# Experts' output rows scattered to their token's place by the experts' pass, and plain reads in the two combines

## The reference

```python
x = x + gnn_0(layernorm(x), edge_attr, src, dst, ...)     # gather, segment sum, MLP
x = x + moe_0(layernorm(x))    # 16 experts, 256 -> 512 -> 256, ReLU, two choices, then a layer norm
x = x + gnn_1(layernorm(x), src, dst, ...)                # dense product, 32 largest kept, mean over neighbours
x = x + moe_1(layernorm(x))    # 8 experts, 256 -> 256 -> 256, GELU, two choices
```

```python
h = act(x @ w1[e] + b1[e]);  y = h @ w2[e] + b2[e]
out = x + w_first * y_first + w_second * y_second
```

## Time and profile before

| | before |
|---|---|
| median of the runs | 2162.16 us (2155.62 to 2167.88) |
| span of the profiled execution | 2148.3 us, mean granted TensorE clock 0.786 |
| PE, PE weight load, VectorE busy | 1334.0, 1159.6, 730.7 us |
| ACT, Pool busy | 427.2, 1088.9 us |
| packets on Pool's software queue | 48192, 131.35 MB, 21.6% of 16 engines |
| packets on SP's hardware queue | 178994, 154.64 MB, 22.3% of 16 engines |
| expert pass e0 | 816 to 1073 us |
| combine and dense product m0 | 1073 to 1262 us |
| expert pass e1 | 1909 to 2062 us |
| last combine o1 | 2062 us to the end |

### The profile page before, as it was taken

The page is one execution under the profiler, slowest core; times in us unless marked ns, Lnnn a source line. Parts: engine busy times, 40 slices in busy tenths (PEclk is TensorE's granted clock), DMA queues, the critical chain, the costliest instruction groups (busy, mean ns, idle before and its releaser), DMA issues. The chain is left out here.

```text
span 2148.3 us, 31218 instructions
## 1 busy us (share of the span) xinstructions
PE 1334.0 (62%) x7997; PEld 1159.6 (54%) x7998; DVE 730.7 (34%) x2198; ACT 427.2 (20%) x1492; POOL 1088.9 (51%) x1144
## 2 busy tenths in 40 slices
PE   0467778788778727999946534454555555358820
PEld 0456667777667716999812224454454454357720
DVE  4123334434434552111169931222222222341123
ACT  0001111111111202444344400000000000114433
POOL 2655556655555103222187746666666666233355
PEclk9878887877888858999956677667677766679975
DMA  5333333333333107999822223333333333139955
GB/s 169 103 99 101 101 99 107 109 97 103 103 100 105 35 8 270 354 349 351 279 82 80 68 64 88 91 96 96 98 88 94 94 97 87 42 112 320 318 175 155
DMA packets 230143, 289.43 MB, mean 135 GB/s; under 512 B 76686, under 2 KB 181152, under 8 KB 229782
## 3 DMA queue, kind: packets, MB, share of 16 engines
q1 hardware_dynamic: 178994, 154.64, 22.3%
q0 software_dynamic: 48192, 131.35, 21.6%
q10 hardware_dynamic: 2852, 2.24, 0.4%
HBM read 256.41 MB, written 32.04 MB: 134 GB/s over the span
## 5 line engine op out<-in xcount | busy, mean ns | idle before, releaser
L726 POOL DMA_INDIRECT O0G<-n_rows,O0idx x392 | 384.2, 980 | 309.1 <-ACT O0idx L721 203.4
L726 POOL DMA_INDIRECT O1G<-sparse_rows,O1idx x392 | 376.7, 961 | 214.4 <-issue 108.2
L739 PE MATMUL O1ps_sums<-O1OH,O1G 128*128 128x128 f32 x1568 | 280.4, 347 | 148.6 <-DVE O1OH L744 84.1
L739 PEld LDWEIGHTS O1ps_sums<-O1OH,O1G 128*128 128x128 f32 x1568 | 259.5, 256 | 163.1 <-DVE O1OH L744 91.0
L739 PE MATMUL O0ps_sums<-O0OH,O0G 128*128 128x128 f32 x1568 | 243.5, 317 | 34.3 <-DMA O0G<-n_rows,O0idx 16.1
L739 PEld LDWEIGHTS O0ps_sums<-O0OH,O0G 128*128 128x128 f32 x1568 | 229.7, 230 | 39.9 <-issue 39.7
L758 DVE TENSOR_TENSOR sumT<-sumT,O1ps_sums 128x256 f32 x98 | 41.3, 421 | 421.6 <-DMA m0own<-token_rows 307.3
L1331 POOL DMA_INDIRECT e0xs<-token_rows,e0idx x64 | 60.5, 946 | 206.2 <-ACT e0idx L1391 205.1
L758 DVE TENSOR_TENSOR sumT<-sumT,O0ps_sums 128x384 f32 x98 | 54.3, 555 | 248.4 <-remote 172.0
L1354 PE MATMUL e0ps_h<-e0xT,e0W 128*128 128x128 f32 x1024 | 128.3, 280 | 0.7 <-DMA e0W<-in_L_ffn_w 0.7
L1354 PEld LDWEIGHTS e0ps_h<-e0xT,e0W 128*128 128x128 f32 x1024 | 122.8, 196 | 1.1 <-DMA e0W<-in_L_ffn_w 1.1
(11 more groups left out here) (300 smaller groups left out, 2078.0 us busy)
## 6 DMA issues: line engine op xcount, KB each, us to landing
e0W<-in_L_ffn_w SPq DMA_DIRECT2D x128, 512.0 KB
e1W<-in_L_ffn_w SPq DMA_DIRECT2D x112, 256.0 KB
O0EA<-in_edge_attr SPq DMA_DIRECT2D x97, 128.0 KB
expert_out<-e0ys SPq DMA_DIRECT2D x64, 128.0 KB
expert_out<-e1ys SPq DMA_DIRECT2D x56, 128.0 KB
O0G<-n_rows,O0idx POOLq DMA_INDIRECT x392
O1G<-sparse_rows,O1idx POOLq DMA_INDIRECT x392
n_rows<-NR SPq DMA_DIRECT2D x5, 640.0 KB
```

The costliest lines, as they stand in the source:

```text
L726: pool.indirect_dma_start(out=self.G[:, s, k, :], out_offset=None, in_=self.rows_dram, in_offset=bass.IndirectOffsetOnAxis(ap=self.idx[:, ...
L739: last = nc.tensor.matmul(self.ps[s % 2][:, h * P:(h + 1) * P], rows, self.OH[:, s, k, :], start=(k == 0), stop=(k == GC - 1))
```

## The change

The rows of a block no longer go to `expert_out` in the block's order. `expert_out` has two rows for each token, 2t + k for choice k, and Pool scatters each block's 128 result rows there by an indirect DMA. For this the routing turns round 2t + k + 1 instead of t + 1, keeps `place` = 2t + k of each row, and derives `token` (half of it) and `dest` (the place, or a number out of bounds for a padding row, which the DMA skips). The combines read a tile's 256 rows as one plain DMA of 2 KB per partition, on SP. `slot` is no longer kept, ACT's index copies are gone in both kinds of step, and Pool has no clearing, no gathers and in o1 no work at all. The two rows of each of the 75 padding tokens are cleared once at the start. Pool's part of the expert pass is written out block by block instead of in a loop, so that an index is a fixed column of `token` or `dest`.

```diff
-    ys_dram = nc.dram_tensor("expert_out", [XS_ROWS, D], F32, kind="Internal").ap()
+    y_dram = nc.dram_tensor("expert_out", [2 * NPAD, D], F32, kind="Internal").ap()
...
+                sp.wait_ge(s_zero, 1)
+                sp.dma_start(y_dram[2 * N:2 * NPAD, :].rearrange("(p k) d -> p (k d)", k=2), sumT[0:NPAD - N, 0, 0:2 * D]).then_inc(s_tail, 16)
...
-                nc.gpsimd.tensor_scalar(row_1[:], rowid[:], 1.0, None, ALU.add)
+                for k in range(2):
+                    nc.gpsimd.tensor_scalar(place_1[:, :, k], rowid[:], 2.0, float(k + 1), ALU.mult, ALU.add)
...
-                    nc.vector.tensor_scalar(token[:, 0:NB], ps_c[:, 0:NB], 1.0, 0.0, ALU.subtract, ALU.max)
+                    nc.vector.tensor_scalar(unused[:], ps_c[:, 0:NB], 0.5, float(NO_ROW), ALU.is_lt, ALU.mult)
+                    link(nc.vector.tensor_scalar(place[:], ps_c[:, 0:NB], 1.0, 0.0, ALU.subtract, ALU.max))
+                    nc.vector.tensor_scalar(token[:, 0:NB], place[:], 1, None, ALU.arith_shift_right)
+                    nc.vector.tensor_tensor(dest[:, 0:NB], place[:], unused[:], ALU.add)
...
         def experts(tag, E, F, NB, w1, b1_cols, w2, b2, func):
...
                 @block.sync
-                    def store(b, s):
-                        sp.wait_ge(y_ready, b + 1)
-                        sp.dma_start(rows_of(ys_dram, b), ys[:, s, :]).then_inc(stored[s], 16)
...
                 @block.gpsimd
                 def _(pool):
-                    def body(i, first):
-                        for s in range(BU):
-                            hold(pool, "pool", idx_ready, i * BU + s + 1)
-                            pool.indirect_dma_start(out=xs[:, s, :], out_offset=None, in_=token_dram,
-                                                    in_offset=bass.IndirectOffsetOnAxis(ap=idx[:, s:s + 1], axis=0)).then_inc(rows_in[s], 16)
-                        if first:
-                            nc.gpsimd.memset(sumT[:], 0.0)
-
-                    in_loops(pool, body)
+                    def fetch(b):
+                        s = b % BU
+                        if b >= BU:
+                            pool.wait_ge(turned, b + 1 - BU)
+                        pool.indirect_dma_start(out=xs[:, s, :], out_offset=None, in_=token_dram,
+                                                in_offset=bass.IndirectOffsetOnAxis(ap=token[:, b:b + 1], axis=0)).then_inc(rows_in[s], 16)
+
+                    def put(b):
+                        s = b % BU
+                        pool.wait_ge(y_ready, b + 1)
+                        pool.indirect_dma_start(out=y_dram, out_offset=bass.IndirectOffsetOnAxis(ap=dest[:, b:b + 1], axis=0),
+                                                in_=ys[:, s, :], in_offset=None, bounds_check=2 * NPAD - 1, oob_is_err=False).then_inc(placed[s], 16)
+
+                    for b in range(BU):
+                        fetch(b)
+                    nc.gpsimd.memset(sumT[:], 0.0)
+                    for b in range(NB):
+                        if b + BU < NB:
+                            fetch(b + BU)
+                        put(b)
+                    for s in range(BU):
+                        pool.wait_ge(placed[s], NI * 16)
...
                 @block.scalar
-                            if not last:
-                                index(b + BU, s, False)
...
                 @block.vector
-                                dve.wait_ge(stored[s], i * 16)
+                                dve.wait_ge(placed[s], i * 16)
...
         class Mix:
-            def gather(self, pool, t, s):
-                hold_tile(pool, "pool", self.idx_ready, t)
-                for k in range(2):
-                    pool.indirect_dma_start(out=self.Y[:, s, k, :], out_offset=None, in_=ys_dram,
-                                            in_offset=bass.IndirectOffsetOnAxis(ap=self.idx[:, s, k:k + 1], axis=0),
-                                            bounds_check=self.NB * P - 1, oob_is_err=False).then_inc(self.gathered[s], 16)
-
-            def load_own(self, sp, t, s):
+            def load(self, sp, t, s):
                 wait_tile(sp, self.once, t, TU)
                 sp.dma_start(self.own[:, s, :], rows_of(token_dram, t)).then_inc(self.own_in[s], 16)
+                wait_tile(sp, self.twice, t, TU)
+                sp.dma_start(self.Y[:, s, :, :].rearrange("p k d -> p (k d)"),
+                             y_dram[ds(t * (2 * P), 2 * P), :].rearrange("(p k) d -> p (k d)", k=2)).then_inc(self.both_in[s], 16)
```

More of the change, by code:

```diff
@@ L1386, in _ @@
                 def _(act):
-                    def index(b, s, first):
-                        if not first:
-                            act.wait_ge(turned, b + 1 - BU)
-                        nc.scalar.activation(idx[:, s:s + 1], token[:, ds(b, 1)], ACT.Copy).then_inc(idx_ready, 1)
                     def xT_copy(b, s, first):
@@ L1413, in body @@
                                 xT_copy(b + 1, (s + 1) % BU, first and s < BU - 1)
-                            if not last:
-                                index(b + BU, s, False)
                             hidden(b, s, first)
-                    for s in range(BU):
-                        index(s, s, True)
                     xT_copy(0, 0, True)
@@ L1440, in build, with __init__ @@
         class Mix:
-            def __init__(self, tag, c, NB):
+            def __init__(self, tag, c):
                 self.Y = sb(tag + "Y", [P, TU, 2, D], F32, c)
                 self.own = sb(tag + "own", [P, TU, D], F32, c)
-                self.idx = sb(tag + "gidx", [P, TU, 2], I32, c)
-                self.gathered = [held_sem(f"{tag}gathered{u}") for u in range(TU)]
+                self.both_in = [sem(f"{tag}both_in{u}") for u in range(TU)]
                 self.own_in = [sem(f"{tag}own_in{u}") for u in range(TU)]
@@ L1449, in __init__ @@
                 self.w = sb(tag + "w", [P, TU, 2], F32, c)
-                self.cleared, self.idx_ready, self.w_ready, self.scaled, self.once, self.twice = (
-                    sem(tag + n) for n in ("cleared", "idx_ready", "w_ready", "scaled", "mixed_once", "mixed_twice"))
-                self.NB = NB
-            def clear(self, pool):
-                nc.gpsimd.memset(self.Y[:], 0.0).then_inc(self.cleared, 1)
-                pool.wait_ge(self.cleared, 1)
-            def indices(self, act, t, s):
+                self.w_ready, self.scaled, self.once, self.twice = (
+                    sem(tag + n) for n in ("w_ready", "scaled", "mixed_once", "mixed_twice"))
@@ L1514, in _ @@
                 def _(pool):
-                    mixer.clear(pool)
                     def step(at):
-                        if x := at(0):
-                            mixer.gather(pool, *x)
                         if x := at(1, True):
@@ L1538, in step @@
                         if x := at(0):
-                            mixer.load_own(sp, *x)
+                            mixer.load(sp, *x)
                         if x := at(5):
@@ L1552, in step @@
                         if x := at(0):
-                            mixer.indices(act, *x)
+                            mixer.weights(act, *x)
                         if x := at(1, True):
@@ L1755, in last_sums @@
                 H = sb("o1H", [P, TU, D], F32, c)
-                mixer = Mix("o1", c, NB1)
+                mixer = Mix("o1", c)
                 s_res, s_out = sem("result_ready"), [sem(f"out_stored{u}") for u in range(TU)]
                 block = c.enter_context(nc.Block())
-                @block.gpsimd
-                def _(pool):
-                    mixer.clear(pool)
-                    def step(at):
-                        if x := at(0):
-                            mixer.gather(pool, *x)
-                    tile_steps(pool, step, 0)
                 @block.scalar
@@ L1802, in _ @@
                     for u in range(TU):
-                        mixer.load_own(sp, u, u)
+                        mixer.load(sp, u, u)
                     with sp.Fori(1, IT) as i:
@@ L1806, in _ @@
                             store(i * TU + u - TU, u)
-                            mixer.load_own(sp, i * TU + u, u)
+                            mixer.load(sp, i * TU + u, u)
                     for u in range(TU):
```

34 lines of the change are left out of this document (16 added, 18 removed).

## The result

The changed kernel takes 2210.27 us (median of four runs, 2196.03 to 2217.11) against 2162.04 us for the kernel before on the same chip: a ratio of 1.018, 95% interval 1.0137 to 1.0222. It is slower, by 48 us. (In one set of the experiments the chip did every kernel some 250 us faster, so the times of that set are compared only within it.) The forecast was 2188 us in a range of 2136 to 2240; the sum had +26 us.

A forecast was written before the change was run, and what follows sets the result against it. It took PE and the DMA engines as near full in e0, PE as busy 126 of 153 us in e1. 17 + 46 + 3 - 13 - 27 = +26 on a 2148 us span gave 2174, 2188 as median; range 2136 to 2240.

The forecast's parts named there:

- o1: Last combine: Pool's gathers go, SP reads plainly, 2.0 us a tile instead of 2.98; -27 us.
- The sign: Whole kernel: slower with chance 0.65, same 0.15, faster 0.20.
- e0: First expert pass: 4.01 us a block, 0.28 more on 60 blocks; +17 us.
- The loop: Expert passes: a fetch stands behind an earlier result and scatter; three blocks take 7.74 us (e0) or 5.99 (e1) plus L.
- L: Expert passes: time from the end of a fetch's generation until PE can start on its rows; 4.3 us e0, 4.0 e1.
- e1: Second expert pass: 3.33 us a block, 0.89 more on 52 blocks; +46 us.
- rival 1: Faster: L falls towards 2.27 us as e1 slows, and e0's loop is covered; -21 us, 2141 us; chance 0.20.
- The edges: Ends of each expert pass: last scatter +1.3 us, routing steps +0.6, earlier first fetch -0.5; +3 us for both passes.
- m0: First combine with the dense product: a plain SP read replaces Pool's clearing and gathers; -13 us.
- Rival 2: Slower yet: SP, with one DMA more per tile, takes o1's gain; +23 instead of -27, 2238 us; chance 0.18.
- Rival 3: Slower yet: waits pull PE's clock to 0.8 in e0 (+39 us) and e1 (+10); 2237 us; chance 0.10.
- Rivals 1 and 4: The fourth: no difference; wait hidden in e0, some 30 us lost in e1, m0 and o1 give 30; chance 0.10.

The follow-up runs named there:

- The two versions with a longer loop: Changed kernel with each scatter one or two blocks later in Pool's order: 2173.52 us (ratio 1.0032) and 2181.35 us (1.0088).
- the version with places in e0 only: First expert pass scatters one block late, first combine reads plain tiles; second pass and last combine as in the kernel before: 1903.41 us (0.9956).

## Why the prediction was right and where it was not

**The sign and the size.** Slower was right. The stages that the change touches cost 38 us in the profiled executions, 37 us between the medians in the quick condition, and 48 us between those of the first comparison, where the forecast had 26. The first graph stage, which no version alters, ended at 763 us in the trace of before, at 784 in that of after and in between in the nine experiments of that condition; so part of the first comparison's 48 us may be this, and the length of that stage should not be trusted to better than 20 us.

**e0: +17 forecast, +21 measured, and the cause shown.** The loop's sum was 7.74 + 4.3 = 12.04 us for three blocks. Over 52 blocks of the trace of after the parts are 4.23 us from transpose to result, 1.34 to the scatter's start, 1.32 to the fetch's, 5.25 to the transpose: 12.14. L, without the fetch's 0.97, is 4.3 as taken. It doesn't come evenly: most results stay 3.7 us apart and every few blocks one comes 0.3 to 3.5 us late, and the last ten blocks carry more. The two versions with a longer loop show it: 233.5 and 234.6 us, where the kernel before has 233.5.

**e1: +46 forecast, +49 measured, the sum right by two errors, the cause only half the story.** The parts are 3.36, 1.48, 1.32 and 4.07: 10.23 us, where 10.0 were summed. L is 3.1 and not 4.0. The DMA engines are less busy once the pass is slower (0.74), and rival 1 had that coming; that this alone sets L is not shown, since the same kernel in the quick condition has 3.6 us at 0.72. The way from transpose to result is 3.36 and not the 2.50 of one block in the earlier trace rows, where a mean over blocks should have been taken. With L at 3.1 and nothing else, the price would have been some 30 us. That the sum is right is luck to that extent. By the waits of the trace in the quick condition the loop alone is enough for the whole loss, though no run took the loop away there; in the usual condition there is a second limit beside it.

**What failed.** The step that failed is the one that priced the scatter on Pool's queue by its generation and gap (1.02 + 0.30 us) and counted nothing more for a second indirect DMA per block. In the chip's usual condition e1 takes 3.2 to 3.4 us a block with that second one, be it scatter or gather, waited for or not, as much as the loop does; so taking away the loop gives back 4 us, where the prediction's sum would have given back all but 5. What the traces show in its place is that engines start late on work that is ready, with two indirect DMAs per block (29 of 56 results by more than 0.6 us where VectorE waits for nothing else, 14 to 21 in the other runs) and not with one (none or one). Why they do, and that this is the whole of the second limit, is not shown. The rows were there: two gathers per tile in the last combine took 2.98 us with 2 x 1.3 us of Pool's own work, though that mean holds two distances of 8.5 and 7.8 us between results.

Of the page's rule ("DMA: Bandwidth & Descriptors" in the Trainium skill, Anatomy of one DMA — SWDGE (gpsimd) path), by which L would be an estimated 2.3 us at any load: the traces have 3.1 in e1 and 4.3 in e0, and the measurements decide.

**The edges: +3 forecast, +13 measured.** Behind e0's and e1's last result Pool closes its block with a DRAIN. In the kernel before and in the changed one (ns min/median/max, first and last start):

```profile
L1269 POOLq DRAIN  x2: 7808/8465/9122, 1051.1 to 2046.5; - x2
```

```profile
L1280 POOLq DRAIN  x2: 1864/5537/9210, 1115.0 to 2149.1; - x2
```

Before, it began 13 to 19 us ahead of the last result, since the last gather was four blocks old, and nobody saw its 8 to 9 us. After, Pool has the last scatter to do: in e1 the drain starts at 2149.1, behind the landed scatters, and the next stage waits out its 9.2 us. In e0 it took 1.9 us; why these two differ no run tells. That an engine's end of block would be long, and covered until now, was in no row of the prediction.

**m0: -13 forecast, -12 measured. o1: -27 forecast, -34 measured.** In the changed o1 a tile took (2206.1 - 2164.3)/24 = 1.74 us by VectorE's last addition, less than the 2.0 us taken from SP's quick rounds and near the 1.8 of the bytes:

```profile
L1766 DVE TENSOR_TENSOR o1H<-o1H,X x25: 424/424/426, 2164.3 to 2206.1; 128x256 f32<-128x256 f32 x25
```

**The rivals.** Rival 2 is out: with Pool's gathers gone from o1, SP's reads took 0.33 to 0.43 us each and none of its rounds was slow. Its slow rounds went with the indirect DMAs beside them and with the usual condition: with the gathers back in o1 in the quick condition, results were at most 3.6 us apart. Rival 3 is out for the changed kernel, e0 (0.99) and e1 (0.94). Rivals 1 and 4 named a real effect, the falling L, but not the second limit.

**Open.** Why engines start late when indirect DMAs come close, and why one chip shows it in one set of runs and not in another half an hour later, no run tells. Neither was it tried whether e1 stays slow in the quick condition with two full indirect DMAs per block and no loop; that no start was late there in the changed kernel speaks against it. If not, the version with the scatter one block later would be some 23 us faster than the kernel before there (an estimate: 12 + 34 gained, 13 lost at the ends and 10 in e1); in the usual condition it is 6 and 11 us slower by the medians of its two measurements. And the version with places in e0 only was measured in the quick condition alone.

## What to carry to other kernels

When two kinds of work share an in-order queue, put the one that waits for a result far enough behind the one that others wait for: one block of delay was worth 21 us in e0 for a change of a few lines. As a first guess, price an added indirect DMA by the mean distance at which the trace already shows them follow each other (here 1.66 us in the first graph stage, so 3.3 us for two), and not by its own duration or by the smallest distance. And give each half of a change its own place: the scatter pays where the pass has room for it (e0 with m0: -8 us or 0.4%, measured in the quick condition, the one complete version here that beat both kernels), and costs where the pass runs near the pace of the gathers (e1).

## What was not expected of the hardware

Indirect DMAs of 128 rows follow each other at a median of 1.25 us in the graph stages. In the condition that all three chips of the experiments were in at some time, engines there often start 0.6 us or more after the work that they wait for is done, and Pool pauses for 3 to 7 us; the mean distance is then 1.66 us in the first graph stage (1.28 in the quick condition), and the gathers of the two graph stages take 147 and 82 us longer, most of the difference between 1912 and 2167 us. With the scatter one block later, e0 has a scatter or gather every 1.9 us on average, and kept 3.7 us a block in both conditions. And Pool's closing drain took 1.9 to 9.2 us behind the expert passes.
